# Latent attention loops: the output product of a pair of heads issued after the next scores instead of before them

## What is computed

```python
q_r    = einsum('bshq,hqr->bhsr', q_big, W_qr)
k_r    = einsum('bld,hdr->bhlr', kv_rope, W_kr)
scores = einsum('bhsr,bhlr->bhsl', q_r, k_r)        # 256 x 512 for each batch and head
attn   = softmax(scores, axis=-1)
ctx_c  = einsum('bhsl,bld->bhsd', attn, kv_rope)    # the product over keys
out    = (ctx_c @ w_kc_kv^T, all heads) @ Wo.T      # added to x; a layer norm follows
```

## Time and profile before

| | |
|---|---|
| median of 3 runs | 3113.54 us (3113.46 to 3119.7) |
| profiled execution, its own time | 3119.23 us |
| its span, first to last instruction | 3117.4 us |
| TensorE matmul busy | 2500.4 us, 80% of the span |
| VectorE busy | 1751.0 us, 56% |
| ScalarE busy | 998.2 us, 32% |
| GpSimd busy | 777.3 us, 25% |
| latent loops (first score to last add) | 901 to 1143, 2157 to 2399 and 2676 to 2918 us |

### The profile page before, as it was taken

The page is one execution under the profiler, slowest core; times in us unless marked ns, Lnnn a source line. Parts: engine busy times, 40 slices in busy tenths (PEclk is TensorE's granted clock), DMA queues, the critical chain, the costliest instruction groups (busy, mean ns, idle before and its releaser), DMA issues. The chain is left out here.

```text
span 3117.4 us, 37690 instructions
## 1 busy us (share of the span) xinstructions
PE 2500.4 (80%) x14394; PEld 1660.1 (53%) x14394; DVE 1751.0 (56%) x3524; ACT 998.2 (32%) x2275; POOL 777.3 (25%) x570
## 2 busy tenths in 40 slices
PE   7786334577999979686868878688998987999899
PEld 4554322124335556466747666574555956455555
DVE  5436587894345652575674846643665864466411
ACT  3032011451035531133333333333554222455310
POOL 1220001000038843210000100002885000588322
PEclk8787565698999989777887978789999976999999
DMA  1000000003000010200010000012001003000311
GB/s 33 18 20 21 0 0 13 0 0 102 0 1 1 1 56 1 110 14 15 4 24 1 14 15 14 14 32 64 1 1 41 1 20 95 1 1 1 112 34 37
DMA packets 96555, 72.86 MB, mean 23 GB/s; under 512 B 51232, under 2 KB 89936, under 8 KB 95801
## 3 DMA queue, kind: packets, MB, share of 16 engines
q1 hardware_dynamic: 95353, 69.01, 7.9%
q0 software_dynamic: 1024, 1.45, 0.2%
HBM read 65.17 MB, written 5.28 MB: 23 GB/s over the span
## 5 line engine op out<-in xcount | busy, mean ns | idle before, releaser
L2017 POOL TENSOR_SCALAR work<-work,small 128x512 f32<-128x512 f32 x384 | 594.3, 1565 | 709.9 <-DVE small L1952 708.4
L1995 ACT ACTIVATE work<-psum,small 128x512 f32<-128x512 f32 x384 | 260.6, 683 | 254.5 <-DVE small L1947 254.5
L1947 DVE TENSOR_REDUCE small<-psum 128x2 f32<-128x1024 f32 x192 | 234.7, 1224 | 175.9 <-PE psum L1897 175.9
L1897 PE MATMUL psum<-keysT,arena_a 64*128 64x512 f32 x768 | 219.2, 650 | 8.9 <-ACT work L1995 6.0
L1907 PEld LDWEIGHTS psum<-consts,work 128*128 128x128 f32 x1536 | 165.4, 141 | 114.1 <-issue 102.5
L1919 PE MATMUL psum<-work,keys 128*64 128x256 f32 x1536 | 187.0, 384 | 36.5 <-issue 34.2
L1907 PE MATMUL psum<-consts,work 128*128 128x128 f32 x1536 | 211.3, 280 | 3.7 <-DVE work L1958 2.6
L1919 PEld LDWEIGHTS psum<-work,keys 128*64 128x64 f32 x1536 | 120.0, 136 | 136.4 <-issue 110.4
L2847 PE MATMUL psum<-xnT,arena_a 128*128 128x256 f32 x512 | 155.9, 466 | 29.7 <-DVE arena_b L3227 29.7
L2847 PEld LDWEIGHTS psum<-xnT,arena_a 128*128 128x128 f32 x512 | 117.8, 238 | 57.3 <-DVE arena_b L3227 32.1
L2820 POOL TENSOR_TENSOR work<-arena_b 128x512 f32<-128x512 f32 x32 | 33.3, 1041 | 439.4 <-ACT arena_b L3108 408.4
(11 more groups left out here) (592 smaller groups left out, 5014.8 us busy)
## 6 DMA issues: line engine op xcount, KB each, us to landing
arena_a<-in_L_xattn_Wo SPq DMA_DIRECT2D x3, 2048.0 KB, 14.9
arena_a<-in_L_xattn_Wq SPq DMA_DIRECT2D x3, 2048.0 KB, 12.8
arena_a<-in_L_xattn_w_kc_q SPq DMA_DIRECT2D x3, 1536.0 KB, 12.5
arena_a<-in_L_attn_w_qkv SPq DMA_DIRECT2D x1, 4096.0 KB
arena_a<-in_L_xattn_W_qr SPq DMA_DIRECT2D x3, 768.0 KB
arena_b<-in_L_ffn_w_fc SPq DMA_DIRECT2D x1, 2048.0 KB
arena_b<-in_L_ffn_w_proj SPq DMA_DIRECT2D x1, 2048.0 KB
arena_a<-in_L_attn_w_gate SPq DMA_DIRECT2D x1, 2048.0 KB
```

Of the source, the lines that this page charges most:

```text
L1897: mm = nc.tensor.matmul(ps[:, u % 2 * 2 + j, :], qT[r:r + DC, p, t * P:(t + 1) * P], k.keysT[r:r + DC, b * SK:(b + 1) * SK], start=True, s ...
L1947: nc.vector.tensor_reduce(top[:, 2 * u:2 * u + 2], ps[:, u % 2 * 2:u % 2 * 2 + 2, :], AX.X, ALU.max, negate=True).then_inc(*maxed.up())
L1995: nc.scalar.activation(probs[u % NPB][:, j, :], ps[:, u % 2 * 2 + j, :], ACT.Exp, bias=top[:, i:i + 1], accum_out=total[:, i:i + 1]).then_ ...
L2017: nc.gpsimd.tensor_scalar(probs[u % NPB][:, j, :], probs[u % NPB][:, j, :], total[:, i:i + 1], None, ALU.mult).then_inc(*scaled.up())
```

## The change

In the lists of two engines, for all three latent loops. TensorE: `output` is taken from even steps, behind `turn`, and put into the following odd step, between `scores` and `over_keys`. VectorE: `add` (and its statistics) is taken from the even step and put at the end of the following odd step.

```diff
-            for s in range(U + LAG + 4):
+            for s in range(U + LAG + 6):
                 if s < U:
                     scores(s)
+                if s % 2 == 1 and 0 <= (s - LAG - 4) // 2 < U // 2:
+                    output((s - LAG - 4) // 2)
                 if s % 2 == 1 and 0 <= (s - LAG - 2) // 2 < U // 2:
                     over_keys((s - LAG - 2) // 2)
                 if 0 <= s - LAG < U:
                     turn(s - LAG)
-                if s % 2 == 0 and 0 <= (s - LAG - 3) // 2 < U // 2:
-                    output((s - LAG - 3) // 2)
...
-            for s in range(U + LAG + 5):
+            for s in range(U + LAG + 6):
                 if s < U:
                     row_max(s)
...
-                q = (s - LAG - 3) // 2
-                if s % 2 == 0 and 0 <= q < U // 2 and q % HP == HP - 1:
+                q = (s - LAG - 4) // 2
+                if s % 2 == 1 and 0 <= q < U // 2 and q % HP == HP - 1:
                     add(q // HP)
```

## The result

The changed kernel takes 3121.86 us (median of 20 runs, 3117.92 to 3129.17), the kernel before beside it 3112.29 us (20 runs, 3107.72 to 3121.42). The ratio is 1.0032, with a 95% interval from 1.0024 to 1.0040: 0.32% slower, 10 us, with an interval from 7.5 to 12.4 us. The time lies in the predicted range, 3112 to 3125. But the forecast was 5.1 us more (3118.6), which the prediction called "no difference", and that is half of what came. The case "slower by over 0.2%", given 0.31, is the one that happened.

A forecast was written before the change was run, and what follows sets the result against it. Loops bound by a closed 7.38 us cycle through TensorE, VectorE and ScalarE, not by TensorE alone. Moved `output` 0, moved adds 9 x 0.57 = 5.1 us on the 3113.54 median gave 3118.6 us, range 3112 to 3125.

The forecast's parts named there:

- no difference: Whole kernel: 5.1 us slower, 0.16%, under the about 0.2% (6.2 us) that a measurement can tell; the same had chance 0.62.
- slower by over 0.2%: Whole kernel: measured time more than 6.2 us above the kernel before; chance 0.31.
- The cycle: Latent loops: even scores, row maximum, exponentials, ScalarE's keep, `over_keys`, `turn` form a closed chain of 7.38 us, the whole period.
- the gap as a wait for the keep: TensorE before `over_keys`: the idle 0.39 us each period is a wait for ScalarE's keep, standing behind two exponentials.
- the signs: Changed profile: gap 0.35 to 0.4 us, period 7.37 to 7.38, odd row maximum 0.9 us earlier, nine periods 7.9 to 8.0.
- Gain of the moved output 0: Part 1, TensorE in the loops: `output` behind the odd scores is on no leg of the period, so gain 0.
- `output` followed by `over_keys`, 0.96: TensorE's new order: 0.96 us for this leg, within 4.12 us from even scores to `over_keys`, leaving a 0.36 us gap.
- The adds on the cycle: Part 2, VectorE's odd step: add and statistics delay the even row maximum by 0.57 us, nine times, 5.1 us.
- the cover of 0.81 us: VectorE's idle time between keep and even row maximum, claimed to hide 0.81 of the add and statistics' 1.40 us.
- rival 3: Slower than can be overlooked: larger remainder per add at batch ends, from 0.69 us up, at most 3126.1 us; chance 0.16.
- the gap is filled: TensorE before `over_keys`: the 0.39 us is a scores-to-`over_keys` switching price that `output` removes; 3081 or 3109 us; chance 0.08.
- the adds cost nothing: VectorE at batch ends: the add's delay is taken up or slips into idle time, 3113.5 us; chance 0.16.

## Why the prediction was right or wrong

- **The cycle, and the gap as a wait for the keep: right.** Moving the exponentials behind the keep took 0.46 us from each of the 87 periods, and an extra row maximum put its 1.13 us into one. Of the signs, the period stayed at 7.37, and the odd row maximum came 0.9 us earlier (0.86 us behind the start of the keep, 986.17 - 985.31 in the changed kernel, for 995.04 - 993.30 = 1.74).
- **Gain of the moved output 0: right**, for the reason given; ratios of 1.0009 and 1.0003 with the add out of the way. The size of the gap left was wrong. The prediction had 0.36 to 0.39 and it is 0.20, because "`output` followed by `over_keys`, 0.96" was read from the loop's end, where `output` stands behind `turn`. Behind scores it takes 1.07. With a shorter cycle this is a loss of 0.19 us in each pair, as the run with the keep first and the moved output shows.
- **The adds on the cycle: right in place and number, 9 x 0.57 us predicted, 0.46 or 0.47 measured nine times.** The mis-sized term is the cover of 0.81 us. I took the keep to hold VectorE for its whole length, 0.69; but the add starts 0.61 after the keep's start (975.36 - 974.75), so that the cover was 0.89. The rows of before already showed such an overlap: the keep starts at 993.30, before the reciprocal's end at 993.38. The three instructions then hold VectorE for 1.38 us (976.74 - 975.36) instead of 1.40. Long periods of 7.9 to 8.0 us and gaps of about 1 us were forecast; they are 7.83 or 7.84, with a gap of 0.66. Predicted 5.1 us, measured 4.2.
- **"So 9 x 0.57 = 5.1 us" as the whole sum: wrong.** The sum had no term for what lies behind the loops, since nothing there is changed. In the profiles it is 2.2 us behind loop 1, 2.3 to 4.6 behind loop 3 and some 1.1 to 1.5 less behind loop 2, and it made the difference between "the same" and "slower". That the range held all the same is its width, which rival 3 had stretched for another reason.
- **The rival "slower than can be overlooked" came true in its sign, not in its mechanism.** Its larger remainder of the adds did not occur (0.46 and not over 0.69); the rest came behind the loops. The rivals "the gap is filled" and "the adds cost nothing" are both out: the period did not fall with the output moved, and with only the add moved the ratio was 1.0035.

## What to carry to other kernels

An engine that is 95% busy need not set the pace: lay the start times of all engines side by side for one period and add up the legs until they close; here only edits of a leg moved the period, and a reordering on ScalarE brought 1.3% where one on TensorE brought nothing. Work that is moved along with a step (here an add and two statistics, once in 16 steps) needs its own look at what stands behind it in its engine's list. Where a busy stretch is followed by a pause, its exact length can move the clock behind it: here by 2 to 5 us behind loops 1 and 3. So repeat a result of that size with another length before believing its cause, and compare the profiles stretch by stretch, those that lie behind the edit too.

## What was not expected of the hardware

Which clock follows behind loops 1 and 3 goes with the length of the loop, to less than a microsecond, alike in all fourteen profiles. Behind loop 3, 225.8, 239.9 to 240.2 and 244.0 us are followed by 201 to 202 us, and 231.5, 240.9 to 241.3 and 244.9 us by 203 to 206 us, for the same work. One extra row maximum in a loop, with all lists else as before, was enough to change the group. And a single pause of TensorE of 2.65 us in the middle of a loop was followed by a stretch at half the clock that cost another 1.6 us, while a pause of 1.52 us in the same place was not.
